# A two-layer graph attention kernel: the memset in front of every gather has 300 columns instead of 332

## What is computed

```python
h = jnp.maximum(_layernorm(x), 0.0)
x = x + gat(h, W, att, bias)            # layer 0
h = jnp.maximum(_layernorm(x), 0.0)
x = x + attention(h, edge_attr, ...)    # layer 1

# layer 0, for every edge (src -> dst), with h = (x @ W.T) in 8 heads
e = leaky_relu(a_src[src] + a_dst[dst], 0.2)
p = exp(e - segment_max(e, dst)[dst])
out = segment_sum(p / segment_sum(p, dst)[dst] * h[src], dst)

# layer 1
score = sum(q[dst] * k[src], -1) / 4 + edge_attr @ We + be
p = exp(score - segment_max(score, dst)[dst])
out = segment_sum(p / (segment_sum(p, dst)[dst] + 1e-8) * v[src], dst) @ Wo + bo
```

## Time and profile before

| | us |
|---|---|
| median of three runs | 1520.3 |
| the three runs | 1502.91, 1520.3, 1521.98 |
| profiled execution, its own time | 1507.14 |
| span of the profiled execution, first to last instruction | 1505.4 |
| POOL busy | 1213.3 (81%) |
| PE busy | 954.2 (63%) |
| DVE busy | 931.1 (62%) |
| ACT busy | 635.1 (42%) |

### The profile page before, as it was taken

How to read it: one execution, slowest core, us unless ns; L and a number is a source line. 1 busy time by engine, 2 the same in 40 slices (tenths; PEclk the granted TensorE clock), 3 DMA queues, 4 the chain that set the end, 5 groups by cost and what they waited for, 6 DMA issues and landing times.

```text
span 1505.4 us, 21963 instructions
## 1 busy us (share of the span) xinstructions
PE 954.2 (63%) x4985; PEld 801.6 (53%) x4985; DVE 931.1 (62%) x3002; ACT 635.1 (42%) x1699; POOL 1213.3 (81%) x1806
## 2 busy tenths in 40 slices
PE   5546575756657575755575667576666667676775
PEld 4335464545545454634454566465555556575654
DVE  6446565665656565656753666566666666666668
ACT  5624344343434343442168244434434444434404
POOL 5888888888888888886038888888888888888820
PEclk9656655666555666566597687777878777776765
DMA  6222222221222222222133333333333333333211
GB/s 140 70 68 47 68 47 67 47 68 47 67 47 69 47 66 47 62 46 82 49 107 88 87 89 88 88 88 88 89 88 90 88 88 88 88 88 88 86 31 43
DMA packets 54209, 110.41 MB, mean 73 GB/s; under 512 B 16876, under 2 KB 30848, under 8 KB 53956
## 3 DMA queue, kind: packets, MB, share of 16 engines
q0 software_dynamic: 36288, 91.12, 23.2%
q1 hardware_dynamic: 16483, 17.39, 4.2%
q10 hardware_dynamic: 1313, 0.50, 0.1%
HBM read 100.60 MB, written 8.81 MB: 73 GB/s over the span
## 4 chain that ended last, share of the span: by engine, by line
POOL 38%; issue 6%; DVE 5%; PE 3%; ACT 1%; DMA 0%; DVEq 0%; POOLq 0%; SPq 0%; ACTq 0%
POOL G L493 28%; POOL pad_i L479 10%; PE bank L826 2%; DVE halves L1048 1%; DVE acc L1402 1%; DVE mv L1055 0%; DVE G L1542 0%; DVE hn L1550 0%; DVE xs L1496 0%; DVE hn L1495 0%; DVE hn L1494 0%; PE bank L873 0%; ACT hn L547 0%; DVE G L1539 0%; DVE hn L1493 0%
## 5 line engine op out<-in xcount | busy, mean ns | idle before, releaser
L493 POOL DMA_INDIRECT G<-table,idx_all x880 | 869.0, 988 | 143.1 <-issue 120.2
L826 PE MATMUL bank<-PV,S 128*125 128x144 f32 x1760 | 435.4, 406 | 105.2 <-DVE PV L1379 83.6
L826 PEld LDWEIGHTS bank<-PV,S 128*125 128x125 f32 x1760 | 361.9, 279 | 134.1 <-issue 120.2
L1402 DVE TENSOR_TENSOR acc<-acc,bank 125x144 f32 x880 | 260.5, 296 | 175.7 <-PE bank L826 113.8
L479 POOL MEMSET pad_i<- 1x332 int32 x880 | 321.5, 365 | 17.6 <-DMA table<-h0b 8.8
L597 ACT ACTIVATE S<-iota_n,lid 128x125 f32<-128x125 f32 x880 | 275.7, 386 | 0.7 <-DVE pen L1143 0.7
L810 PE MATMUL bank<-qe,ST 125*128 x880 | 150.3, 325 | 57.7 <-DVE prod L1199 41.8
L810 PEld LDWEIGHTS bank<-qe,ST 125*128 125x128 f32 x880 | 132.4, 230 | 67.4 <-issue 66.5
L1379 DVE TENSOR_TENSOR PV<-G,PV 128x512 f32<-128x512 f32 x220 | 150.8, 686 | 18.9 <-issue 18.8
L601 ACT ACTIVATE S<-S,ones 128x500 f32<-128x500 f32 x220 | 156.6, 712 | 7.2
L607 ACT ACTIVATE ST<-bank 125x512 f32<-125x512 f32 x110 | 66.8, 607 | 218.8 <-PE bank L797 141.7
(11 more groups left out here) (220 smaller groups left out, 1241.7 us busy)
## 6 DMA issues: line engine op xcount, KB each, us to landing
G<-table,idx_all POOLq DMA_INDIRECT x880
prod<-in_edge_attr_dram SPq DMA_DIRECT2D x8, 672.0 KB
table<-G SPq DMA_DIRECT2D x12, 224.0 KB
bias_rows<-qe SPq DMA_DIRECT2D x1, 1664.0 KB, 5.8
table<-h0b SPq DMA_DIRECT2D x8, 178.5 KB
out_dram<-G SPq DMA_DIRECT2D x8, 168.0 KB
prod<-in_edge_attr_dram SPq DMA_DIRECT2D x8, 90.0 KB
xs<-in_x_dram SPq DMA_DIRECT2D x1, 504.0 KB
```

The costliest lines, as they stand in the source:

```text
L493: pool.indirect_dma_start(G[:, u, v, 0:w], None, table, bass.IndirectOffsetOnAxis(ap=idx_all[:, g * GV + v:g * GV + v + 1], axis=0)).then_ ...
L826: last = pe.matmul(sums_bank(p)[0:BN, at:at + H * SLOT], S[:, ur, v, :], PV[:, v, :, :].rearrange("p h k -> p (h k)"), start=True, stop=True)
L1402: ve.tensor_tensor(a, a, o, ALU.add).then_inc(s.sem["acc_added"], 1)
```

## The change

The width of the memset ahead of each gather goes from 332 to 300 columns, at the one call that both layers use. The scratch `pad_i` keeps its size; order, waits and semaphores are the same.

```diff
                         for v in range(QV * j, QV * j + QV):
-                            space(332)
+                            space(300)
                             pool.indirect_dma_start(
                                 G[:, u, v, 0:w], None, table,
```

## The result

| | before | after |
|---|---|---|
| median, us | 1516.25 (four runs, 1502.91 to 1521.98) | 1573.21 (four runs, 1564.45 to 1581.71) |
| profiled execution, us | 1507.14 | 1576.14 |
| span, us | 1505.4 | 1574.4 |

The ratio is 1.0391, 95% interval 1.0331 to 1.0451: the kernel became 3.9% slower. The forecast was a gain of 1%; it has the wrong sign, and the time lies outside its range. The stages say where the time went: from the first gather to the last addition layer 0 took 697.5 us before and 714.5 after (17 more), layer 1 690.5 and 742.3 (52 more); together the 69 us between the spans.

A forecast was written before the change was run, and what follows sets the result against it. POOL was taken to set the pace in both layers: 864 x 26.6 ns = 23.0 us, cut by holds to 8 + 11 = 19 us. Against the median 1501, called 1500 us; forecast range 1485 to 1515, 8 in 10 within 1480 to 1530.

The forecast's parts named there:

- The memset: POOL's memset ahead of each gather: 300 columns should take 338.4 ns, 26.6 less, 297.8 us in all instead of 321.5.
- Every hold's end is fixed by DVE: Long gathers at L493 end a set time behind a two-input DVE instruction, so savings ahead of them are given back.
- the ledger: Count per layer 0 group: only eight memsets behind the last hold save, 0.21 us of 0.43; 5.8 us over 27 groups.
- The 19 us of the sum: Expected gain on POOL after holds: 8 us in layer 0 plus 11 in layer 1, against a plain 23.0.
- the second half of the Trainium skill's rule: SBUF lock: a gather that came first would make DVE wait some 0.9 us; the row of 1361.50 shows 0.1.
- If everything else on POOL keeps its length: Condition on the plain sum for POOL: 864 gathers on the path x 26.6 ns = 23.0 us.
- DVE's 2.4 us of waiting a group covers the 0.43 us: Layer 1: DVE's wait for gathers exceeds what a group shortens, so POOL keeps setting the pace.
- (c): Rival at L493: the gather itself lengthens once the pause ahead shrinks; 1550 to 1577 us, chance 0.11.
- The sign named for a wrong forecast: On POOL: the prediction is wrong if POOL starts to wait for `pv_ready`, the semaphore by which L1379 reports.
- (a): Rival: larger holds of gathers vanish in both layers; 38 us less, 1482 against the median; with other lost holds, chance 0.11.
- (b): Rival: holds of gathers give the saving back in full; 1520 (1507 to 1520) us, chance 0.14 with small losses.

The follow-up runs named there:

- l0only: Memset of 300 columns in layer 0 alone, 332 kept in layer 1, against the kernel before, chip A: 1496.0 us, ratio 0.9941.
- w316: Memset of 316 columns instead of 332 in both layers, against the kernel before: 1496.3 us (0.9966) on chip A, repeated on chip C at 1494.8 us (0.9943).
- none: No memset between the gathers, against the kernel before with 332 columns, chip B: 1788.6 us, ratio 1.1795.
- w308again: Memset of 308 columns instead of 332, a repeat on chip B, against the kernel before: 1546.9 us, ratio 1.0228.

## Why the prediction was wrong, point by point

**The memset: right.** 338 ns were worked out and 338 measured, 297.2 us in all against 297.8.

**Every hold's end is fixed by DVE, and what was saved ahead of it is given back: right, where the course stayed regular.** A group of l0only that answers to that of the earlier trace rows, timelines of POOL and then of DVE:

```profile
234.62 1.12 POOL L493 DMA_INDIRECT G<-table,idx_all  x1 [0.16 <-issue]
...
237.68 1.48 POOL L493 DMA_INDIRECT G<-table,idx_all  x1 [0.16 <-issue]
...
239.65 1.14 POOL L493 DMA_INDIRECT G<-table,idx_all  x1 [0.16 <-POOL pad_i L479]
```
```profile
234.58 0.40 DVE L1276 TENSOR_TENSOR_SCAN FR<-pcur,smax 128x128 f32<-128x128 bf16 x1
...
237.65 0.67 DVE L1379 TENSOR_TENSOR PV<-G,PV 128x512 f32<-128x512 f32 x1
...
239.56 0.48 DVE L1326 TENSOR_TENSOR_SCAN FF<-pcur,CC,smax 128x128 f32<-128x128 bf16 x1
```

The large hold still ends 0.84 behind L1379 (239.16 and 238.32), the first 0.76 behind L1276, the gather of L1379 starts 26 ns behind it (the ledger had 35), and lasts 1.48 instead of 1.42. The first and third grew from 1.03 and 1.12 to 1.12 and 1.14. At L493 layer 0 is busy for 440.0 us in l0only, 21 above 440 x 0.952, where before has 17.7 of excess: 3 more, where 5 were expected. The ledger gave 5.8 us for layer 0 (11.5 without it); the medians give 6.1, the ratio 4.7 to 13.1, which fits the ledger and doesn't exclude 11.5. w316 got 5.9 and 7.7 of 11.5, mixed 11.8 and 13.3 of 23.0: about half again, for both layers together. The 19 us of the sum was on the high side, for it took 8 and 11 where half is 11.5.

One row was misread on the way. At 1361.50 L1379 started 40 ns ahead of the gather, so the row says nothing of a gather that came first. The trace of before has other cases: in layer 0 L1379 starts 78 times while a gather runs, and takes 672 to 695 ns each time. DVE isn't held by a gather that was there before it, and the second half of the Trainium skill's rule that the prediction cites finds no support here.

**"If everything else on POOL keeps its length": it did.** The gather kept its 0.95 us, and it delivered as soon: from the start of a quarter's first gather to the first move of its semaphore the median is 2.24 us in layer 0 and 2.43 in layer 1 before, 2.23 and 2.42 after.

**"DVE's 2.4 us of waiting a group covers the 0.43 us [...], so no other engine takes over": the step that failed.** It compares POOL's saving with DVE's reserve and takes DVE's and TensorE's steps as given lengths. They are not: at the faster pace TensorE's increments come up to 8.8 us late, and the steps of layer 0, 24 us each in before, take 18 to 35. The range had no term for it. Before has 41 late increments, 63 us in sum, and stays regular; after has 236, 683 us in sum. Nothing in the earlier trace rows shows that, since a wait that ends late looks like a wait; it is seen only by setting a waiting instruction's start beside the end of what it waited for.

**The rivals.** (c) had the sign and the size (1550 to 1577), and not the mechanism: it put the loss at L493, whose busy time fell. The sign named for a wrong forecast, that POOL starts to wait for `pv_ready`, is what came, 69.3 us of it. It was written without a cost or a chance of its own; a rival "the chain behind POOL loses its regular course" belonged there, for the 2.4 us of layer 1 made it the nearest engine. (a) and (b) didn't come into play.

**What stays open.** What holds TensorE's increments back, and why only TensorE's. In after 73 of the 218 late moves come 0.2 to 0.4 us behind a gather's start and in none most come once POOL has stopped, which ties them to the stream of gathers; how, no run shows. Whether many late increments break the regular course or the broken course makes them: w308again tips in mid-layer under unchanged instructions, and regular runs near the edge (mixed, l0only) already have 56 and 59 in layer 0, before 11, which speaks for the first, but shows it not. What differs between chips: at distances of 1.447 to 1.458 B is slow, and A (in one layer, or as a mean) and C (as a mean) were not at 1.447. The exact case of the change, 300 in both layers, ran only on B and in the measurement of the result, so how it would do on A or C isn't known. A rule of the Trainium skill stands near this (VectorE: DVE Perf Modes, The TRN2 errata — SBUF-src ops pay a fixed extra latency per instruction): it warns that "high-rate event-accel sem-incs from one engine can deadlock another", and that kernels with dense increments from several engines should space them. No run here stood still; whether the lateness seen here is a mild form of that, no run tells.

**The version to keep.** mixed, 204 columns at the first gather of a quarter and 332 at the other three, was faster than before on A and C, by 0.5% and 0.8% (clear of the noise by its intervals, though small); the changed kernel wasn't run there; it wasn't tried on B, where distances of 1.458 and less cost 2 to 4%. The fall beside it is steep.

## What to carry to other kernels

A delay that looks idle may hold a pace at which everything else runs smoothly; before shortening it, try it longer and shorter at two or three sizes and on more than one chip, since the loss can come at an edge and not by the nanosecond. When the engine that sets the pace gets faster, don't only compare its saving with its followers' reserve: see how late each follower starts behind the end of what releases it, now and after. If an engine that never waited begins to wait for a buffer, the cause is downstream, and the first late start there is the place to look.

## What the runs showed of the hardware that was not expected

- TensorE's hand-over to DVE takes 36 to 38 ns in the pair L873 to L1309 of before, and up to 5.5 us in after; over all pairs of after DVE's waits reach 8.3 us. It goes with the pace of another engine's indirect DMAs: at gathers 1.503 us apart 41 late ones in the two layers, at 1.451 (both on chip B) 239.
- The semaphore itself moves late, by the trace's own record of its moves, and TensorE's alone: those of DVE and ACT that ended such waits stand at most 13 ns behind the instruction's end, in before, after and none.
- Fewer rows don't help: gathers of 96 rows take 931 ns instead of 952, come more often, and cost more (1634.6 against 1567.5 us, some 10 of them a memset).
- One program has two courses. The text of l0only took 0.6% less than before on one chip and 1.7% more on another, and one run changed from one to the other in mid-layer.
